# Ten extra matrix products per image tile in the window attention of a fused embedding kernel

## The reference, cut to what matters

```
x = patches @ patch_w + patch_b;  x = layernorm(x) + position;  identity = x
x = gelu(x @ ff1_w + ff1_b) @ ff2_w + ff2_b
q, k, v = split(x @ qkv_w + qkv_b)
scores = q @ k.T / 4                      # per image and head: 64 x 64
x = (softmax(scores) @ v) @ proj_w + proj_b + identity
x = x + ff(x)                             # same ff as above
h = concat(x, text_embedding)             # 64 image + 128 text tokens, 8 times
h = h + attention_and_linear_attention_block(layernorm(h))
h = h + mixture_of_experts(layernorm(h))  # 16 routed experts, top 2, and 2 shared
```

## Time and profile before

| | us |
|---|---|
| three timed runs | 967.78, 970.87, 975.27 |
| their median | 970.87 |
| the profiled execution, its own time | 966.41 |
| its span, first to last instruction | 964.7 |
| TensorE busy | 861.0 |
| VectorE / ScalarE / GpSimd busy | 297.6 / 258.4 / 210.2 |
| mean granted clock of TensorE | 0.910 |

### The profile page before, as it was taken

The page is one execution under the profiler, slowest core; times in us unless marked ns, Lnnn a source line. Parts: engine busy times, 40 slices in busy tenths (PEclk is TensorE's granted clock), DMA queues, the critical chain, the costliest instruction groups (busy, mean ns, idle before and its releaser), DMA issues.

```text
span 964.7 us, 17607 instructions
## 1 busy us (share of the span) xinstructions
PE 861.0 (89%) x7060; PEld 626.3 (65%) x7060; DVE 297.6 (31%) x739; ACT 258.4 (27%) x547; POOL 210.2 (22%) x269
## 2 busy tenths in 40 slices
PE   5569988947888898898889999999999999999998
PEld 4224575623556466466574756569988999999754
DVE  0135162054445455454434054111111111111134
ACT  0211111313354544544532320112121212122111
POOL 5653110024523123123001004400000000000162
PEclk9769556967799999998889899999999999999999
DMA  9900000030000000000000003108878788877422
GB/s 282 336 21 0 1 1 1 1 141 7 1 1 2 1 2 2 1 2 2 2 1 1 0 1 143 62 16 312 306 275 295 269 301 286 301 289 289 144 79 62
DMA packets 34170, 102.28 MB, mean 106 GB/s; under 512 B 5139, under 2 KB 20275, under 8 KB 28740
## 3 DMA queue, kind: packets, MB, share of 16 engines
q1 hardware_dynamic: 22884, 67.05, 19.1%
q10 hardware_dynamic: 5616, 23.01, 7.2%
q0 software_dynamic: 5616, 11.46, 3.7%
HBM read 90.30 MB, written 11.21 MB: 105 GB/s over the span
## 4 chain that ended last, share of the span: by engine, by line
PE 70%; DVE 8%; issue 7%; DMA 6%; POOL 3%; ACT 3%; another core or an unknown queue 1%; SPq 1%; ACTq 0%; DVEq 0%; POOLq 0%
PE PS L1326 18%; PE PS L1920 10%; PE PS L1828 7%; PE PS L1924 5%; DMA w_rgu<-in_wgu 5%; PE PS L1842 5%; PE PS L1830 4%; PE PS L1435 2%; PE PS L1332 1%; PE PS L1538 1%; PE PS L1655 1%; PE PS L1571 1%; PE PS L1425 1%; PE PS L1402 1%
## 5 line engine op out<-in xcount | busy, mean ns | idle before, releaser
L1920 PE MATMUL PS<-xt,w_rgu 128*128 128x128 f32 x936 | 112.3, 276 | 5.4 <-DMA w_rgu<-in_wgu 3.2
L1920 PEld LDWEIGHTS PS<-xt,w_rgu 128*128 128x128 f32 x936 | 108.6, 192 | 9.7 <-issue 7.7
L1291 DVE TENSOR_TENSOR rh<-rsg,PS 128x768 f32<-128x768 f32 x39 | 37.2, 954 | 225.2 <-ACT rsg L831 225.2
L1326 PE MATMUL PS<-w_rdn,rh 128*128 128x192 f32 x468 | 82.7, 327 | 1.9 <-issue 1.9
L545 POOL DMA_DIRECT2D y_slots<-ys x39 | 21.1, 542 | 271.0 <-ACT ys L823 271.0
L1326 PEld LDWEIGHTS PS<-w_rdn,rh 128*128 128x128 f32 x468 | 75.1, 190 | 2.3 <-issue 2.2
L831 ACT ACTIVATE rsg<-PS 128x768 f32<-128x768 f32 x39 | 31.6, 810 | 158.8 <-PE PS L1924 158.8
L1828 PE MATMUL PS<-X,w_sgu 128*128 128x512 f32 x144 | 71.1, 616 | 1.7 <-DVE gu L1184 1.6
L1924 PE MATMUL PS<-xt,w_rgu 64*128 64x128 f32 x936 | 62.7, 280 | 0.0
L1924 PEld LDWEIGHTS PS<-xt,w_rgu 64*128 64x128 f32 x936 | 55.3, 187 | 4.7
L460 POOL TENSOR_TENSOR rs<-ve,minus_half 128x3 f32<-128x3 f32 x12 | 10.4, 866 | 186.3 <-DVE ve L1035 186.3
(11 more groups left out here) (311 smaller groups left out, 1425.4 us busy)
## 6 DMA issues: line engine op xcount, KB each, us to landing
w_rgu<-in_wgu SPq DMA_DIRECT2D x39, 1152.0 KB, 7.9
w_rdn<-in_wd ACTq DMA_DIRECT2D x39, 576.0 KB, 4.0
x_slots<-zeros SPq DMA_DIRECT2D x1, 3744.0 KB
xs<-x_slots SPq DMA_DIRECT2D x39, 96.0 KB, 6.9
y_slots<-ys POOLq DMA_DIRECT2D x39, 96.0 KB, 5.2
w_sgu<-in_shared_gu SPq DMA_DIRECT2D x2, 1152.0 KB
patches<-in_patches SPq DMA_DIRECT2D x1, 1536.0 KB
w_tff<-in_w_tff SPq DMA_DIRECT2D x2, 576.0 KB
```

What stands on the lines that cost most here:

```text
L1291: dve.tensor_tensor(rh[:, j, :], rsg[:, j, :], PS[:, 2:4, :].rearrange("p a b -> p (a b)")[:, 0:FF], ALU.mult).then_inc(S["r_h"], 1)
L1326: mm = pe.matmul(dst, lhs, rhs, start=(k == 0), stop=(k == len(pairs) - 1))
L1920: pe.matmul(dst(k, m), w_rgu[:, j, k, 128 * m:128 * m + 128], xt[:, j, k, :], start=(m % 4 == 0), stop=False, skip_group_check=True)
```

## The change

A constant `SPARE` of 10 is added. In the loop over the four image tiles, TensorE now does ten products between the scores of the next tile and the transposes of this one. Each has the full tile of ones, 128 x 128, as its weights, and one 128 x 192 slice of `w_tff2` as its moving operand. All ten write the same 192 columns of bank 4, each starting afresh. Nobody reads them: the transposes of the same tile overwrite them. The wait for ScalarE's copy of the tile before (`a_ptc`), which used to stand behind the wait for the exponentials, now stands ahead of the ten; for the first tile a wait for `a_y` stands there, on which TensorE has waited once already. The wait for the exponentials comes behind the ten.

```
+SPARE = 10
...
             for i in range(IT):
                 if i + 1 < IT:
                     img_scores(i + 1)
-                pe.wait_ge(S["a_exp"], i + 1)
                 if i >= 1:
                     pe.wait_ge(S["a_ptc"], i)
+                else:
+                    pe.wait_ge(S["a_y"], KC)
+                for _ in range(SPARE):
+                    pe.matmul(PS[:, 4, 0:D], ones_sq[:, :], w_tff2[:, 0, :], start=True, stop=True)
+                pe.wait_ge(S["a_exp"], i + 1)
                 for k in range(NH):
```

## The result

The changed kernel took 986.23 us (median of four runs, 984.73 to 988.47), the kernel before 969.33 (four runs, 963.72 to 975.27). The ratio is 1.0175, 95% interval 1.0109 to 1.0241: slower, by 17 us. The profiled execution took 984.73 us, its span is 983.0.

What follows compares the result with a forecast made beforehand. TensorE was taken to bound the kernel, busy 89% of the span and 70% of the chain. 23.5 - 5.4 - 3.2 = +14.9 us on a mean of 970.1 gave 985 us; own range 979 to 991, overall 976 to 992.

Steps and rivals of the forecast that it cites:

- The mechanism in the stage: Image attention, scores of tile 1 to projection start: tens start cold, warm transposes and values; 44.3 us becomes about 59.
- No wait to fill: Image attention: TensorE never waits for the exponentials, so nothing covers the ten products and their head start buys nothing.
- The price of the ten: Each tile: 6 products cold at 0.74 us and 4 warm at 0.36, 5.9 us; four tiles 23.5, bounds 20.5 to 26.6.
- The 0.78 at 64.10 us: Lower-clock price: a product of the same shape starts at 64.10, the next at 64.88; 0.74 us was taken.
- the 0.36: Full-clock price of a product: 48 records of the same shape, two to a product, in 8.6 us busy.
- The rival of cheaper products: Ten products with free weight loads: 0.32 us warm, 0.65 cold, 20.7 in all and +12 us; chance 0.03.
- The clock falls between the tiles: Image attention: thin values and scores between tens let the clock fall, so each later tile's ten start cold again.
- The rival with the clock up: Image attention: the first ten lift the clock and later tens hold it to the projection; +5.5 us, about 976; chance 0.12.
- What it gives back: Warm clock in image attention: transposes save 5.4 us, values 3.2 (bounds 0 to 3.5), scores and projection counted at nothing.
- my reason: Scores gain nothing countable: 48 records in 2.7 us are loads and issue more than columns.
- Behind the stage: Later stages start later; clock dips may move them 2 or 3 us either way; over 3 us behind 193 us means wrong.

Runs made afterwards that it cites:

- either fill: Spare products in two longer waits (34 and 9), or four in the attention-opening pause: changed kernel 970.42 or 977.16 us, kernel before 955.01 or 960.67.

## Why the prediction was right

It gave 985 us, and 986.23 was measured; +14.9 was forecast, and the medians differ by 16.9. The mechanism in the stage was right. That the total came so near is in part luck: the stage cost 2.6 us less than forecast, and a part behind it, forecast at nothing, made up for it.

*No wait to fill.* Right. The ten are on the chain in every tile, and no wait for the exponentials appears or disappears.

*The price of the ten.* 23.5 us forecast, 22.6 measured, out of two errors that cancel. From one to the next a cold product takes 0.64 us and not 0.74, a warm one 0.325 and not 0.36, and the first of each ten brings some 0.2 to 0.3 more. The 0.78 at 64.10 us ran to a product of another shape, with a longer gap before it, and the 0.36 was busy time over four separate groups of products, each with a tail. More of them ran cold than six a tile: 22.6 us make about 27 cold products of 40, not 24. The rival of cheaper products had these prices right (0.32 and 0.65), at a chance of 0.03; the time it gave, +12, was counted within the forecast.

*The clock falls between the tiles.* Right: in every trace it is at 0.50 again before the next tile's spare products begin, mostly by the first of the scores. The rival with the clock up called for later tens of 3.6 us; they took 5.2 to 6.2, and in the run with twenty they still began cold. The rule of the Trainium skill's page "TensorE: Matmul & The Clock Gate" ("Why this matters for your kernels") that ties such falls to long idle gaps does not describe this stage: the longest wait between its first ten and its end is 1.6 us.

*What it gives back.* Transposes 4 x (2.71 - 1.32) = 5.6, forecast 5.4. Values 16.5 - 11.8 = 4.7, forecast 3.2 and at most 3.5: wholly warm they take 2.76 us. I had taken 3.23 for warm, which was partly cold. The scores gave nothing, but because they ran at 0.50; my reason, that they are loads and issue, does not hold, as they gained 0.4 us in the run with ten in tile 0. The projection gave nothing back, as forecast; it lost 0.5. The stage: 22.6 - 5.6 - 4.7 = +12.3, against 14.9.

*Behind the stage.* This step failed as I put it: a change of more than 3 us behind 193 us would prove me wrong, and it was 6.1 in the trace. I had put 2 or 3 us either way on it and counted none. In the first traces of both kernels the whole of it is one fall of the clock behind a pause of 1.27 us, in which TensorE's load was nearly the same in both kernels (2.01 and 2.04 us busy); the work behind those records takes as long in both. Why the clock falls there in the one and not in the other is not shown beyond the place of its rise, and that four products in the pause undo it is likely, by the clocks of the executions, and not proved. Its share in the medians is not settled. Two sets give +16.9 and +17.3 for the change, the stage and the projection account for 12.9 and 12.3 in their traces, and with either fill in both kernels the difference is 14.3 or 15.1, each good to some 3.5 us. If before loses its clock there in about half of its executions and the changed kernel in nearly all, as their mean clocks suggest, the fall adds half of 6.2 us to the 12.9: an estimate of 16, near both sets.

## What to carry to other kernels

Products that only warm TensorE's clock must stand where the chain of waits shows TensorE waiting; between two pieces of its own work they cost their full time, here 22.6 us for 10.3 given back. A count of them that ends just as the clock rises is a poor buy: five cost three quarters of what ten did. Look also at how far the warmth reaches: here to the transposes and values of the same tile, and the clock was lost again before the next dense work. Placed in waits of 12.1 and 3.2 us, ahead of dense projections, the same products made the kernel 0.7% faster (ratio 0.9926). And compare more than one trace before a difference far behind the change is put down to it: here 150 records took 12.2 or 18.4 us by whether the clock fell at a pause of 1.27 us.

## What the runs showed of the hardware

Ten products of 16 rows kept TensorE busy for 6.6 us on end at 0.50, and ten of 128 rows and the same columns raised the clock to 1.00 after 3.5 to 5.6 us in the first trace, and after 3 to 6 us over all traces; cold, both kinds cost the same, 0.64 us from one product to the next. The weights being equal ten times over made nothing cheaper: warm, a product cost 0.325 us, as those with different weights do in the feed-forward at 181 us of before.

The transposes (`pe.transpose` in the kernel) do count for the clock: in the first trace it rose right behind those of tiles 1 and 2 with only thin products before them, and in the run with thin products behind those of tiles 1, 2 and 3, though never within a thin ten. In tiles 0 and 3 of the first trace the same transposes did not raise it. The Trainium skill's page "TensorE: Matmul & The Clock Gate", in "Part 4: PE-mode transpose", says that the full clock does not engage for them; here they raised it, and 12 of them took 1.32 us at the upper level and 2.71 at the lower.
